# Making the gate columns of a block's output first, in four lanes, and placing every part of a five-engine schedule anew

## The reference

```python
def rat_write(res, y, wod_w, wab_w, wab_b, du_w, du_b):
    o_d = y @ wod_w.T                    # 512 outputs and 8 low-rank numbers
    A_B = y @ wab_w.T + wab_b            # 48 + 48 + 16 gate columns
    out = o_d[..., :H];  delta_low = o_d[..., H:]
    delta = softplus(delta_low @ du_w.T + du_b)
    A_neg = -softplus(A_logit)
    A_bar = exp(delta * A_neg)
    B_bar = (A_bar - 1.0) / (A_neg - SSM_EPS) * B_proj
    B_bar_skip = delta * B_skip
    return hs * [A_bar, 1] + out * [B_bar, B_bar_skip]
...
x = x + layer(_layernorm(x))             # two rat_writes: after attention, after the MLP
x = x + experts(_layernorm(x))           # 8 experts of rank 16, softmax router
```

## Time and profile before

| | us |
|---|---|
| time, median of three runs | 1636.47 (1634.73 to 1637.02) |
| profiled execution: span, first to last instruction | 1627.3 |
| profiled execution: own total time | not recorded beside the span |
| median less span | 9.2 |
| TensorE busy | 1531.8 |
| VectorE busy | 1129.6 |
| ScalarE busy | 921.9 |
| GpSimd busy | 364.1 |

### The profile page before, as it was taken

The page is one execution under the profiler, slowest core; times in us unless marked ns, Lnnn a source line. Parts: engine busy times, 40 slices in busy tenths (PEclk is TensorE's granted clock), DMA queues, the critical chain, the costliest instruction groups (busy, mean ns, idle before and its releaser), DMA issues.

```text
span 1627.3 us, 25328 instructions
## 1 busy us (share of the span) xinstructions
PE 1531.8 (94%) x9574; PEld 1169.6 (72%) x9574; DVE 1129.6 (69%) x1782; ACT 921.9 (57%) x1702; POOL 364.1 (22%) x346
## 2 busy tenths in 40 slices
PE   7999999999999988899999999899999999999986
PEld 6567666666666656778798778798877898875554
DVE  7777745888888878644463785974776955636777
ACT  5444345888888776455543656643657644552443
POOL 1645555555433420110002000012000011001000
PEclk8999999999999999899999999999999999999998
DMA  9667677999987945356577766667766667756542
GB/s 371 204 254 243 223 181 229 276 293 284 273 233 197 253 138 189 130 185 223 202 218 233 258 226 221 214 218 232 265 233 221 223 197 237 218 180 213 203 178 104
DMA packets 127609, 360.94 MB, mean 222 GB/s; under 512 B 15744, under 2 KB 45056, under 8 KB 111872
## 3 DMA queue, kind: packets, MB, share of 16 engines
q1 hardware_dynamic: 127200, 359.19, 68.7%
q10 hardware_dynamic: 288, 0.13, 0.0%
HBM read 273.15 MB, written 86.11 MB: 221 GB/s over the span
## 4 chain that ended last, share of the span: by engine, by line
PE 74%; DVE 12%; ACT 6%; DMA 3%; issue 3%; POOL 1%; SPq 0%; DVEq 0%; ACTq 0%; POOLq 0%
PE ps L1921 21%; PE ps L1933 9%; PE ps L693 5%; PE ps L1249 5%; PE ps L1236 4%; PE ps L1272 4%; PE ps L1946 4%; PE ps L1879 3%; PE ps L1864 3%; PE ps L1809 3%; ACT a_p L1378 3%; PE ps L1824 3%; PE ps L1891 3%; DMA p_x<-in_x 2%; PE ps L652 2%
## 5 line engine op out<-in xcount | busy, mean ns | idle before, releaser
L1921 PE MATMUL ps<-m_y_split,m_win 128*128 128x512 f32 x1536 | 372.7, 396 | 2.7 <-issue 2.7
L1921 PEld LDWEIGHTS ps<-m_y_split,m_win 128*128 128x128 f32 x1536 | 284.2, 189 | 63.9 <-issue 7.1
L1308 DVE TENSOR_REDUCE a_negmax<-ps 128x1 f32<-128x640 f32 (+7 forms) x176 | 180.7, 1027 | 61.1 <-PE ps L1239 60.3
L1378 ACT ACTIVATE a_p<-ps,a_negmax 128x128 f32<-128x128 f32 (+7 forms) x256 | 188.5, 750 | 36.0 <-DVE a_negmax L1308 33.8
L1933 PE MATMUL ps<-m_wods,m_y_split 128*128 128x316 f32 x768 | 178.7, 322 | 3.8 <-DVE m_hT L2145 3.4
L2183 ACT ACTIVATE m_turned<-ps 128x512 f32<-128x512 f32 x128 | 75.0, 596 | 160.3 <-PE ps L1809 129.1
L1249 PE MATMUL ps<-ident,a_p 128*128 128x128 f32 x1152 | 157.8, 275 | 2.9 <-DVE a_pT L1321 2.0
L1236 PE MATMUL ps<-a_k,a_q 128*128 128x512 f32 (+3 forms) x384 | 124.4, 403 | 16.7 <-ACT a_p L1378 15.0
L1933 PEld LDWEIGHTS ps<-m_wods,m_y_split 128*128 128x128 f32 x768 | 128.5, 192 | 8.0 <-DVE m_hT L2145 3.7
L1249 PEld LDWEIGHTS ps<-ident,a_p 128*128 128x128 f32 x1152 | 123.5, 141 | 5.4 <-DVE a_pT L1321 3.5
L2341 POOL TENSOR_TENSOR m_scale<-m_scale,mhalf 128x2 f32<-128x2 f32 x16 | 13.0, 813 | 493.5 <-DVE m_scale L2081 493.5
(11 more groups left out here) (250 smaller groups left out, 3095.3 us busy)
## 6 DMA issues: line engine op xcount, KB each, us to landing
m_win<-mlp_in_split SPq DMA_DIRECT2D x128, 512.0 KB, 4.4
m_wods<-mlp_out_split SPq DMA_DIRECT2D x96, 316.0 KB, 3.3
p_xT<-in_xT SPq DMA_DIRECT2D x16, 1024.0 KB, 9.9
p_x<-in_x SPq DMA_DIRECT2D x16, 1024.0 KB, 10.6
a_q<-qk_split SPq DMA_DIRECT2D x64, 256.0 KB, 7.0
a_k<-qk_split SPq DMA_DIRECT2D x128, 128.0 KB, 7.2
mlp_in_split<-a_w_two SPq DMA_DIRECT2D x32, 512.0 KB, 5.5
m_hs<-in_x SPq DMA_DIRECT2D x15, 1024.0 KB, 5.6
```

Source lines behind the costliest of these rows:

```text
L1308: V.tensor_reduce(negmax[:, n % 4, 0:len(units[n][3])], by_head(n, score_banks(n)), AX_X, ALU.max, negate=True).then_inc(max_ready, 1)
L1378: m = S.activation(dst[:, j, :], src[:, j, :], ACT.Exp, bias=negmax[:, n % 4, j:j + 1], accum_out=rsum[:, si % 2, q * 4 + hh:q * 4 + hh + 1])
L1921: m = nc.tensor.matmul(bank_of("m", blk, step), win[s][:, wl, ic, :], y[k], start=(ic == 0 and p3 == 0), stop=(ic == HCH - 1 and p3 == 2))
```

## The change

- Block 3 gets 68 steps: after the 32 input steps come four (`ABS`) which make the 120 low-rank and gate columns of all four tiles in one PSUM bank, five k-chunks a step (5, 5, 5 and 1), from runs of 120 numbers; VectorE adds the bias at the last of them into four new tiles `ab_last`. Then the 32 output steps, in the same two rounds, with 512 columns only. The four tiles' outputs go to banks 0, 2, 3 and 1. Turn, low, delta and output of other parts get banks 6, 7, 0 and 2 from the second round on.
- The writes of tiles 12 to 15 have a table of their own (`L`) and four lanes (1, 0, 2, 4; hidden-state tiles 0, 4, 5, 1). In `scale` they do the first skip product, `scaled` and `less_one`, none of which needs the output; `x` comes next; `sum` is the rest: `skip_out`, `skip_end`, `times_out` and `sum`.
- The expert layer waits for x and for the sum. ScalarE's moments use a new tile `spare`, and an x load waits for the addition before (`x2_ready`).
- Room for the new tiles comes from a smaller DMA scratch area of GpSimd's queue (`dynamic_dma_scratch_size`), which this kernel issues nothing from.
- All positions are new, in all blocks; the experts of tiles 12 to 15 have their own table (`F`).

```diff
-PLACES = {...
- 'W': {'load': -0.03, 'low': 0, 'delta': 1.26, 'gates': 2.51, 'loadx': 3.16, 'scale': 4.46, 'sum': 5.28, 'x': 6.73},
...
+PLACES = {'L': {'load': -2.22,
+                 'low': -1.18,
+                 'delta': 0.59,
+                 'gates': 3.0,
+                 'loadx': 3.77,
+                 'scale': 3.94,
+                 'x': 5.24,
+                 'sum': 14.03},
...
+           'F': {'mean': 10.05,
+                 'turn0': 10.92,
+                 'turn1': 11.54,
+                 'spread': 13.76,
+                 'turn2': 14.18,
+                 'down0': 13.17,
+                 'down1': 13.36,
+                 'turn3': 14.39,
+                 'down2': 15.8,
+                 'down3': 16.6,
+                 'router': 16.19,
+                 'weigh': 17.18,
+                 'lowT': 18.55,
+                 'out0': 22.24,
+                 'out1': 22.99,
+                 'out2': 23.57,
+                 'out3': 26.04,
+                 'store': 20.85},
...
- 'w': {...
-       12: 240,
-       13: 243.3,
-       14: 256,
-       15: 258},
+           'w': {...
+                 9: 202.97,
+                 10: 221.41,
+                 11: 229.73,
+                 12: 235.8,
+                 13: 240.1,
+                 14: 246.89,
+                 15: 251.97},
...
+           'e': {...
+                 9: 204.29,
+                 10: 221.6,
+                 11: 230.44,
+                 12: 240.47,
+                 13: 245.91,
+                 14: 254.32,
+                 15: 258.8},
...
+        spare = sb("e_spare", [P, D])
+        ab_last = [sb(f"m_last_ab{j}", [P, ABW + 1]) for j in range(TB)]
...
         m_x.append(sb("m_last_x", [P, D]))
+        assert place[0] <= ahead_end
+        place[0] = last_place[1]
+        Ab.append(sb("m_last_A", [P, NA * HS]))
+        delta.append(sb("m_last_delta", [P, H]))
+        tmp.append(sb("m_last_tmp", [P, H]))
+        g1.append(sb("m_last_gate", [P, 4, NA]))
+        dlT.append(sb("m_last_lowT", [P, P], F32R))
...
+        LAST = NT - TB
+        ABK = 5
+        ABS = -(-MCH // ABK)
+
+        def down0(blk):
+
+            return 32 if SPLIT[blk] else 32 + ABS
+
+        placed += [(64 * blk + step, ("m", blk, step, None)) for blk in range(NBLK) for step in range(down0(blk) + 32)]
...
-                        lane, h = ((1, 0), (0, 4), (1, 1), (0, 5))[i % TB]
+                        lane, h = ((1, 0), (0, 4), (2, 5), (4, 1))[i % TB]
...
-            if what == "m" and part >= 32 and (part - 32) % MCH == 0:
-                r = (part - 32) // MCH
+            if what == "m" and part == 32 and not SPLIT[i]:
+                one.plan(("d", i, None, 1), 1, readers=TB)
+            if what == "m" and part >= down0(i) and (part - down0(i)) % MCH == 0:
+                r = (part - down0(i)) // MCH
                 for q2 in ROUNDS[i][r]:
                     if SPLIT[i]:
                         one.plan(("d", i, q2, r), q2, readers=1 + r)
                     else:
-                        one.plan(("d", i, q2, 0), 2 * (q2 % 2))
-                        one.plan(("d", i, q2, 1), 2 * (q2 % 2) + 1)
-            if what == "m" and (i, part) == (NBLK - 1, 63):
+                        one.plan(("d", i, q2, 0), (0, 2, 3, 1)[q2])
+            if what == "m" and (i, part) == (NBLK - 1, down0(NBLK - 1) + MCH):
+                one.banks = [6, 7, 0, 2]
+            if what == "m" and (i, part) == (NBLK - 1, down0(NBLK - 1) + 2 * MCH - 1):
                 one.banks = [6, 7, 0, 1, 2, 3]
...
+            elif k < down0(i):
+                c0 = ABK * (k - 32)
+                cn = min(ABK, MCH - c0)
+                move(w2[s][:, 0:cn * ABW].rearrange("p (k c) -> p k c", k=cn),
+                     wod2T[c0:c0 + cn, :, H:WOD].rearrange("k p c -> p k c")).then_inc(wt_loaded[s], 16)
-                    move(w2[s][:, :], wod2T[c]).then_inc(wt_loaded[s], 16)
+                    move(w2[s][:, 0:H], wod2T[c][:, 0:H]).then_inc(wt_loaded[s], 16)
...
                 pe.wait_ge(x2_ready, i + 1)
+                pe.wait_ge(hs_ready, nth("sum", "w", i))
                 turn_quarter("e", i, q)
...
+            if step < down0(blk):
+                if step == 32:
+                    wait_for_bank(pe, "d", blk, None, 1)
+                k0 = ABK * (step - 32)
+                for k in range(k0, min(k0 + ABK, MCH)):
+                    wait_for_emptied(pe, "m", blk, up_step(k))
+                    for q in range(TB):
+                        m = nc.tensor.matmul(bank_of("d", blk, None, 1)[:, ABW * q:ABW * q + ABW],
+                                             hT[:, k, P * q:P * q + P], w2[s][:, ABW * (k - k0):ABW * (k - k0) + ABW],
+                                             start=(k == 0 and q == 0), stop=(k == MCH - 1 and q == TB - 1))
+                m.then_inc(wod2_mm, 1)
+                return
+            r, k = divmod(step - down0(blk), MCH)
             tiles = ROUNDS[blk][r]
             if SPLIT[blk]:
                 pe.wait_ge(hlo_ready, MCH * sum(SPLIT[:blk]) + k + 1)
             if k == 0:
                 for q in tiles:
                     wait_for_bank(pe, "d", blk, q, 0)
-                    wait_for_bank(pe, "d", blk, q, 1)
-            wait_for_emptied(pe, "m", blk, up_step(k))
             for q in tiles:
-                for c0, cn, b in ((0, H, 0), (H, ABW, 1)):
-                    m = nc.tensor.matmul(bank_of("d", blk, q, b)[:, 0:cn], hT[:, k, P * q:P * q + P],
-                                         w2[s][:, c0:c0 + cn], start=(k == 0), stop=(k == MCH - 1))
+                m = nc.tensor.matmul(bank_of("d", blk, q, 0), hT[:, k, P * q:P * q + P], w2[s][:, 0:H],
+                                     start=(k == 0), stop=(k == MCH - 1))
                 if q == tiles[-1] or k == MCH - 1:
                     m.then_inc(wod2_mm, 1)
...
             if step == "skip":
                 bs = ab_t[:, DR + 2 * NA:ABW].unsqueeze(1).broadcast_to([P, HS, RH])
                 dve.wait_ge(dve_own.sem, own_at[what, i])
+                own_at[what, i] = dve_own.then_inc(V.tensor_tensor(
+                    tmp[k][:, :].rearrange("p (s r) -> p s r", s=HS),
+                    delta[k][:, :].rearrange("p (s r) -> p s r", s=HS), bs, ALU.mult))
+            if step == "skip_out":
+                dve.wait_ge(dve_own.sem, own_at[what, i])
                 if what == "w":
                     wait_for_emptied(dve, "d", i // TB, i % TB, 1 if SPLIT[i // TB] else 0)
                 else:
                     wait_for_emptied(dve, what, i, "out")
-                n = dve_own.then_inc(V.tensor_tensor(
-                    tmp[k][:, :].rearrange("p (s r) -> p s r", s=HS),
-                    delta[k][:, :].rearrange("p (s r) -> p s r", s=HS), bs, ALU.mult))
-                dve.wait_ge(dve_own.sem, n)
                 own_at[what, i] = dve_own.then_inc(V.tensor_tensor(tmp[k][:, :], tmp[k][:, :], out_t[:, :], ALU.mult))
             if step == "skip_end":
                 dve.wait_ge(dve_own.sem, own_at[what, i])
...
                 for step in ("gates", "outer", "factor"):
                     write_step(step, what, i)
             if part == "scale":
-                for step in ("skip", "skip_end"):
-                    write_step(step, what, i)
+                if what == "w" and i >= LAST:
+                    dve.wait_ge(hs_loaded[h], hs_loads[what, i])
+                    write_step("skip", what, i)
+                    for step in ("scaled", "less_one"):
+                        write_step(step, what, i)
+                else:
+                    for step in ("skip", "skip_out", "skip_end"):
+                        write_step(step, what, i)
             if part == "sum":
-                for step in ("scaled", "less_one", "times_out", "sum"):
-                    write_step(step, what, i)
+                if what == "w" and i >= LAST:
+                    for step in ("skip_out", "skip_end", "times_out", "sum"):
+                        write_step(step, what, i)
+                else:
+                    for step in ("scaled", "less_one", "times_out", "sum"):
+                        write_step(step, what, i)
             if part == "x":
                 x_at = x_place(i)
-                dve.wait_ge(hs_ready, nth("sum", what, i))
+                if i >= LAST:
+                    dve.wait_ge(dve_own.sem, own_at[what, i])
+                else:
+                    dve.wait_ge(hs_ready, nth("sum", what, i))
                 dve.wait_ge(mx_loaded[x_at], x_loads[i])
                 V.tensor_tensor(hs[h][:, :], hs[h][:, :], m_x[x_at][:, :], ALU.add).then_inc(x2_ready, 1)
...
+            if step < down0(blk):
+                if step == down0(blk) - 1:
+                    dve.wait_ge(wod2_mm, wod2_count[blk, "ab", ABS - 1])
+                    for q in range(TB):
+                        V.tensor_tensor(ab_last[q][:, 1:ABW + 1], bank_of("d", blk, None, 1)[:, ABW * q:ABW * q + ABW],
```

(13 more changed lines are left out.)

343 lines of the change are left out of this document (178 added, 165 removed).

## The result

The changed kernel takes 1607.55 us, median of four runs (1603.77 to 1611.42), beside 1635.6 for the kernel before: a ratio of 0.9838, 95% interval 0.9818 to 0.9857. The profiled execution has a span of 1609.3 us and a time of its own of 1611.42: 2.1 us lie outside the span; in the kernel before run again it is 2.2 (1632.03 and a span of 1629.8). So the traced execution of the kernel before took about 1627.3 + 2.1 = 1629.4 (an estimate), 7 us less than the median of its kernel.

A forecast was written before the change was run, and what follows sets the result against it. TensorE, busy 94% of the span, was taken as the bound until about 1570, then VectorE to 1607. Tile 15's write ending at 1588.7 + 22.1 + 2 + 9.2 outside the span gave 1622.0 us, 14.5 faster; range 1611 to 1632.

The forecast's parts named there:

- All parts placed anew: Ahead of block 3: same work in new order, 0 change taken, bounds 10 us less and 8 us more.
- 29.8 us of idle time: TensorE's idle time from 640 to 1467.3 us, scattered over block boundaries; some could go and some come.
- Rival C: Ahead of block 3: new places also take 10 us from TensorE's idle time, giving 1612 us; chance 11%.
- the end of tile 15's sum: End of the last tile's write: VectorE's work, waits and gaps put it at 1588.7 against 1605.2, 16.5 us earlier.
- 22.1 + 2: After tile 15's write: the last tile's chain of 22.1 us, plus 2 us for TensorE's additional remaining work.
- Narrow products: Block 3's gate and low-rank columns made first: 128 narrow instructions near 0.11 us each, no change in total taken.
- Last output product: End of block 3's output: 7.1 us of other TensorE work moves before it, so it ends at 1571 us.
- TensorE isn't the bound: In the tail: TensorE alone would be done with experts 12 to 15 at 1601.5 us, so it does not bound.
- 9.2 us: Distance of the timed runs' median, 1636.47, from the profiled span, 1627.3; carried over to the forecast time.
- B: Output phase of block 3: VectorE runs late and TensorE waits, losing 8 of 16.5 us: 1630 us; chance 15%.
- D: Tail: bound by ScalarE and two-deep turned tiles, giving back nearly everything: 1636 us; chance 5%.
- E: Output stretch: TensorE waits one for one for VectorE's added 28 us, slower at 1641 us; chance 7%.

The follow-up runs named there:

- new splits: Changed kernel with old positions for everything ahead of block 3, except the sixteen split parts of each block at new positions: 1620.30 us, ratio 0.9917.
- x late: Changed kernel with the x addition of tiles 12 to 15 put behind the sum again: 1617.57 us, ratio 0.9897.
- wide steps late: Changed kernel with x, `scaled` and `less_one` of tiles 12 to 15 all put behind the output: 1630.75 us, ratio 0.9976.
- old turns: Changed kernel with old positions for the opening and for the turns that prepare blocks 1 to 3: 1608.91 us, ratio 0.9837.
- old splits: Changed kernel with old positions for the opening and for the sixteen splits of the hidden product: 1608.60 us, ratio 0.9837.
- old opening: Changed kernel with old places for tiles 0 to 3 after attention and the first block's eight turns: 1606.91 us, ratio 0.9824.

## Why the prediction missed, step by step

The step that failed is "All parts placed anew ... I take 0". It measured -7.6 us in the kernel before and -9.6 in the changed one. I had named the direction as open and the bound as 10 us less, and argued against it with "nothing in the code shortens those chains". What fell is the waits: TensorE's idle time in blocks 0 to 3 went from 20.6 us to 12 (13.4 in the kernel before with the new places), inside the bound, and the busy time of the same instructions by another 1.1 to 4.9 us. The opening, which I had not looked at by itself, took 1 to 5 us back. That the waits got shorter because parts that wait for each other were moved apart in the queues is my reading. It is shown for one wait, the first of block 0's output, which the new splits alone cut from 3.4 to 2.1 us; and even there another wait came in its place until the reads were moved too.

The second part, the clock, could have been seen in the trace of the kernel before, in a window of 10 us behind the wait at the start of block 0's output:

```profile
810.00:820.00 10.00, 10.00 (x47) 8.56 (x46) 9.93 (x10) 1.48 (x3) 0.00 (x0) 0.79 0.53 138
```

TensorE is busy for all of it, and at a granted clock of 0.79. Such slow work isn't in the 29.8 us of idle time from which I took the bounds, and I had read the clock in the tail alone. Rival C, at 11%, said just this, that the new places also take 10 us from the idle time, and had 1612. It came true in direction and nearly in size; its counter-argument was the one I went by, and it was wrong.

The second, smaller miss is in the terms of block 3: the end of tile 15's sum was to come 16.5 us earlier, with 22.1 + 2 behind it, a block 3 and tail of 145.5. Measured are 143.1 and 142.6.
- Narrow products: 13.1 to 14.8 predicted, 14.3 to 14.8 measured. No load stood bare: right. The Trainium skill ("TensorE: Matmul & The Clock Gate", section LDWEIGHTS) puts a load at its columns over 1.2 GHz, 107 ns for 128. One narrow instruction starts every 0.111 us (40 in 4.46 us of the chain), just over that figure. Columns don't set it: 64-column instructions of the same trace cost 0.108 us each, nearly as much as those of 120 or 136. What does, no run here shows; the load is the candidate.

```profile
1466.39 4.46 PE ps L2011 x40
```
```profile
923.16 1.73 PE ps L1942 x16
```

- Last output product: predicted to be over at 1571, it is over at 1567.5, 101.3 us after the first narrow one where 103.7 were predicted. All the parts that I counted in front did come there (in instructions: 96 for 82 of the down products, 24 for 18 of the expert outputs, 56 for 48 of the turns, 45 for 27 of low and delta). But the 1.6 us of idle time that the stretch had before are gone, which I had left in; the other 0.8 are not placed.
- VectorE is busy for 88.40 of the 96.70 us from 1490 to the end of tile 15's sum, 91%, where over 93 was forecast. That end is at 1586.7, 120.5 us after the first narrow product, where 121.4 were predicted; 119.9 in the second trace. It held to 1%, and not by luck: 108.4 us of work and 13 of waits and gaps were added up, 107.9 and 12.6 are measured.
- From there to the end: 22.6 and 22.7, where 24.1 were predicted. "TensorE isn't the bound" was too strong: behind 1571 the chain is TensorE's for 19 us, VectorE waits 2.0 us for it at 1576, and tile 15's turns start at 1587.70, 1.0 us after its sum, behind two expert outputs. It cost 0.5 of the 2 us that I had set aside.
- Tail 42, "about 40" predicted, and no 8.6 us wait. The clock was not 1.0 to near the end: 0.91 from 1567.5 to 1586.7, where TensorE waits 3.3 us for a weighted row.

The 9.2 us "outside the span" were read wrongly: 2.1 lie there, 7 were the distance of the traced execution from the median. As the sum was carried as a difference (-14.5), this cost it nothing.

Together: the gain is 28.0 and 25.4 us by the medians of the two comparisons, 26.5 and 26.8 by their ratios, so 11 to 13.5 more than the 14.5 that were forecast. The places ahead of block 3 account for 7.6 to 9.6 of them, block 3 and tail for 2.4 to 2.9. What is left is within what medians of one kernel differ by here (1607.55 and 1608.63, 1635.6 and 1633.99).

Rivals B, D and E did not occur: no wait of TensorE in the output stretch, ScalarE at 12.38 of 19.20 us at its densest. But x late and wide steps late show E's mechanism as soon as the VectorE work is behind the output: the output stretch grows by 5.9 and 16.0 us. With wide steps late nothing of block 3's gain is left (166.7 against 159.9 before): the gain is the VectorE work put ahead of the outputs, which the narrow products allow but don't bring by themselves.

## What to carry to other kernels

Find the stretch in which an engine has no gaps left; work that can be done ahead of the operand it was queued behind is worth up to its full duration for every tile whose instructions cross into it, not only for the last two (here 8.5 us for 9.2 of work, and 24.1 for 23.2). When a whole table of positions changes, don't put it at zero: take the idle time at the boundaries as what it can win (here 8 of 20.6 us), add the stretches with a granted clock below 1.00, and test it by exchanging the table in both kernels. Positions are tuned as a set; putting back one kind can cost more than putting back all.

## What the hardware showed

The same order of instructions can meet a clock drop in one execution and not in another. Old turns and old splits have the same opening, and 436.6 and 431.1 us for it. The opening and then 5 us of it, old turns first:

```profile
263.30:699.90 436.60, 403.02 (x3454) 284.77 (x3452) 360.53 (x541) 325.41 (x770) 163.24 (x152) 0.97 0.78 225
670.00:675.00 5.00, 5.00 (x19) 4.03 (x19) 1.31 (x6) 1.97 (x2) 0.14 (x1) 0.50 0.00 0
```
```profile
265.30:696.40 431.10, 396.20 (x3454) 279.74 (x3453) 359.38 (x541) 325.75 (x770) 163.55 (x153) 0.98 0.79 227
670.00:675.00 5.00, 5.00 (x24) 3.09 (x24) 3.77 (x8) 2.73 (x6) 0.69 (x1) 1.00 0.49 146
```

TensorE's 3454 instructions are the same, and take 403.02 us in one and 396.20 in the other; its idle time is not longer in old turns (33.6 against 34.9). So the 5.5 us are slow clock. Both traces have slow stretches, but at different times: old turns from 595 to 605 (0.66) and at 670 (0.50), where old splits has 1.00; old splits from 685 to 700 (0.66), where old turns has 0.89. Of ten traces with the old opening eight have 430.4 to 431.1, two 435.6 and 436.6; the eight with the new one have 432.5 to 436.2, so that what the new opening costs is 1 to 5 us and isn't settled. The Trainium skill ("TensorE: Matmul & The Clock Gate", the section on the HAM clock gate) says that the moment at which the clock changes differs from run to run; these two traces agree, and add that a slow stretch can be there in one execution and missing in another. It is a likely reason, not shown further, why medians of one kernel here differ by 1 to 2 us.

The start differed too: attention's first product comes at 261.3 to 266.3 us in the traces, although the compute engines run the same operations in the same order up to there.
